# W_self's first row halves between x's tiles, their low halves on GpSimd, and the first products in another order

## The chip, the cores and the metric

The kernel runs on one core of one Trainium2 chip. The time is the device time of one execution in microseconds (us). The kernel before takes 241.03 us, the median of three runs (240.89 to 241.05). Differences of over 0.2% of that, 0.48 us, count as faster or slower here.

## The reference, cut to what matters

A graph layer over 625 nodes with 512 features and 20,625 edges of 4 kinds:

```python
h = relu(layernorm(x))
msg  = sum over r of (h[src] @ W_rel[r] + b_rel[r]) * where(edge_type == r, edge_weight, 0)
agg  = segment_sum(msg, dst) / max(segment_sum(edge_weight, dst), 1)
x1   = layernorm(h + h @ W_self + b_self + agg) * ln1_g + ln1_b
ffn  = gelu(x1 @ W_ffn1 + b_ffn1) @ W_ffn2 + b_ffn2
out  = x + layernorm(x1 + ffn) * ln2_g + ln2_b
```

Everything is float32. The change lies in the product `h @ W_self` and in what leads to it: the load of x, its row means and its transposition.

## The kernel before, in words

The 625 rows are five tiles of 125 (`c` or `s` from 0 to 4). An operand of a product is split in two float32r parts, a high one (a copy that rounds) and a low one (the rest), and a product is three: high by high, low by high, high by low. The low by low one is left out.

The weights come in units of 512 KB, two blocks of 128 rows of W (`k` = 0 and 1). Unit `u` lands in one of three staging buffers (`stage_view(u)`), ScalarE (ACT) writes its high part into `wring` (`high_part`), and VectorE (DVE) the low part (`low_part`). Units 0 and 1 are W_self; units 2 to 9 are W_rel; then come W_ffn1 and W_ffn2. Unit 0 is treated by itself: its two row halves are two DMAs of 256 KB, and each has its own conversion. The semaphore `first_in` tells that half 0 has landed and `stage_in[0]` that half 1 has; `first_hi`, `w_hi`, `first_lo` and `w_lo` tell of the conversions.

A tile of x goes this way: DVE takes its mean (`row_mean(c)`, three instructions), ACT subtracts it and applies the relu (`h_of(c)`), TensorE (PE) transposes it in four instructions (`turn_h(c)`), ACT writes the high part of the transposed tile (`hT_high(c)`) and DVE the low part (`hT_low(c)`), which give the semaphores `hT_a` and `hT_b`. Each engine does its work in the order in which the program writes it, and waits in that order. On ACT, `h_of(3)` stands behind `hT_high(2)`, and `h_of(4)` behind `hT_high(3)`.

PE starts with ten dummy products on a tile of ones, turns tiles 0 and 1, does three more dummies, and then the 30 products of unit 0, six for each tile, with the other three turns between them. Unit 1 follows at once. In the text a product is named by its two operands (the transposed h first), so high by low is hT's high part by W's low part, and by the row half and the tile: `(k, s)`.

GpSimd (POOL) fills constants until 6.2 us and has nothing to do until the five means are there. The loads are all issued by SyncE (SP), but for the last 13 rows of each tile of x, which ACT issues.

Of the kernel before, what the change touches and what calls it, by code (L numbers as in the profile page):

```python
# [10 lines left out]
ALU = mybir.AluOpType  # L11
# [8 lines left out]
def gnn_layer(nc, x, src, dst, etype, ew, W_self, b_self, W_rel, b_rel, ln1_g, ln1_b, ln2_g, ln2_b,  # L20
# [53 lines left out]
    RING = 2  # L74
    FG = [(0, 3 * TP), (3 * TP, 2 * TP)]
    UB = 6
    WARM = [10, 3]

    SUM_ROWS = [0, 32, 64]
    BK = SUM_ROWS[-1] + TR  # L80
# [96 lines left out]
    with ctx:  # L177
# [112 lines left out]
        def stage_view(u):  # L290
            v = stage[u % STAGES][:, :]
            return v if U_REL <= u < U_W1 else v.rearrange("p (k n) -> p k n", k=2)

        def f32(ap):
            return ap.bitcast(F32)
# [56 lines left out]
        @block.sync  # L352
        def _(sp):

            def load_x(c):
                p0, p1 = SPANS[0]
                sp.dma_start(x1[p0:p1, c, :], x[c * TN + p0:c * TN + p1, :]).then_inc(x_in[c], 16)  # L357

            def load(u):
                if u >= STAGES:  # L360
                    sp.wait_ge(w_lo, u - STAGES + 1)
                sp.dma_start(stage_view(u), units[u][0]).then_inc(stage_in[u % STAGES], 16)

            def sums_by_relation(c):

                sp.wait_ge(A_a, group_of(c, NG - 1))
                sp.wait_ge(A_b, group_of(c, NG - 1))
                if c >= 2:
                    sp.wait_ge(agg_ps, c - 1)
                for row, half in zip(SUM_ROWS, (0, 1, 0)):  # L370
                    sp.dma_start(f32(sums[row:row + TR, c % 2, :]),
                                 f32(AT[c % 2][half][SUMS:SUMS + 1, :, :])).then_inc(sums_in[c % 2], 16)

            for c in range(3):
                load_x(c)
            sp.dma_start(stage_view(0)[:, 0, :], units[0][0][:, 0, :]).then_inc(first_in, 16)  # L376
            sp.dma_start(stage_view(0)[:, 1, :], units[0][0][:, 1, :]).then_inc(stage_in[0], 16)
            for c in range(3, NT):
                load_x(c)
            load(1)  # L380
            sp.wait_ge(tails, 1)
            for f, vec, signal in ((1, dst, dst_in), (3, ew.bitcast(I32), w_in), (0, src, src_in), (2, etype, src_in)):
                flat = vec.rearrange("(p e) -> p e", p=TN)
                sp.dma_start(raw[0:TN, f, 0:EC], flat).then_inc(signal, 16)
                sp.dma_start(raw[0:TN - 1, f, EC:EW], flat[1:TN, 0:EW - EC]).then_inc(signal, 16)
            load(2)
            for buf, vec in ((bself_bc, b_self), (g1_bc, ln1_g), (b1_bc, ln1_b)):
                row = vec.rearrange("(a d) -> a d", a=1)
                sp.dma_start(buf[:, :], row.broadcast_to([P, D])).then_inc(consts_in, 16)
            with nc.allow_non_contiguous_dma("bias by partition"):  # L390
                sp.dma_start(bf1, b1.rearrange("(f p) -> p f", p=P)).then_inc(consts_in, 16)
            sp.wait_ge(blk_iotas, 3)
            for row in SUM_ROWS:
                for r in range(R):
                    sp.dma_start(brel_raw[row + r * NT:row + (r + 1) * NT, :],
                                 b_rel[r:r + 1, :].broadcast_to([NT, D])).then_inc(brel_in, 16)
            for u in range(STAGES, U_REL):
                load(u)
            sums_by_relation(0)
            for u in range(U_REL, U_REL + STAGES):  # L400
                load(u)
            for c in range(1, NT):
                sums_by_relation(c)
            for u in range(U_REL + STAGES, NU):
                load(u)

            sp.wait_ge(agg_ps, NT)
            for c in range(NT):
                for p0, p1 in SPANS:
                    sp.dma_start(x_again[p0:p1, c, :], x[c * TN + p0:c * TN + p1, :]).then_inc(late_in, 16)  # L410
            for buf, vec in ((g2_bc, ln2_g), (b2_bc, ln2_b), (bf2_bc, b2)):
                row = vec.rearrange("(a d) -> a d", a=1)
                sp.dma_start(buf[:, :], row.broadcast_to([P, D])).then_inc(late_in, 16)
            for c in range(NT - 1):
                sp.wait_ge(y_out, c + 1)
                for p0, p1 in SPANS:
                    sp.dma_start(out[c * TN + p0:c * TN + p1, :], ybuf[p0:p1, c % 2, :]).then_inc(out_done[c % 2], 16)
            p0, p1 = SPANS[0]
            for i, (d0, d1) in enumerate(HALVES):
                sp.wait_ge(y_out, NT + i)  # L420
                sp.dma_start(out[(NT - 1) * TN + p0:(NT - 1) * TN + p1, d0:d1],
                             ybuf[p0:p1, (NT - 1) % 2, d0:d1]).then_inc(last_done, 16)
            for i in range(2):
                sp.wait_ge(out_done[i], ROWS_IN * len(range(i, NT - 1, 2)))
            sp.wait_ge(last_done, 16 * 2 * len(HALVES))

        @block.gpsimd
        def _(pool):
            chain = [0]

            def link(ins):
# [29 lines left out]
            g.iota(iota_q[:, :, :], [[K_STEP, TR], [1, SW]], base=0, channel_multiplier=0,  # L461
                   allow_small_or_imprecise_dtypes=True).then_inc(iotas, 1)

            pool.wait_ge(xmean, NT)
            link(g.tensor_scalar(var_e, mv[:, :, 1], EPS, None, ALU.add))
            g.tensor_tensor(rstd, var_e, mhalf, ALU.pow).then_inc(xrstd, 1)
# [11 lines left out]
        def _(act):  # L478
# [12 lines left out]
                    act.wait_ge(agg_ps, NT)  # L491
                a.copy(units[u][1], stage_view(u)).then_inc(w_hi, 1)

            def first_high(k):

                if k == 0:
                    act.wait_ge(first_in, 16)
                    a.copy(units[0][1][:, 0, :], stage_view(0)[:, 0, :]).then_inc(first_hi, 1)
                else:
                    act.wait_ge(stage_in[0], 16)  # L500
                    a.copy(units[0][1][:, 1, :], stage_view(0)[:, 1, :]).then_inc(w_hi, 1)  # L501

            def h_of(c):

# [35 lines left out]
            h_of(0)  # L540
            h_of(1)
            hT_high(0)
            first_high(0)
            hT_high(1)
            first_high(1)
            h_of(2)
            hT_high(2)
            h_of(3)
# [65 lines left out]
        def _(dve):  # L614
# [16 lines left out]
            def row_mean(c):  # L631
                link(row_stats(c))
                link(v.bn_aggr(mv[0:TN, c, :], stats[0:TN, c, :]))
                v.tensor_scalar(nm[0:TN, c:c + 1], mv[0:TN, c, 0:1], -1.0, None, ALU.mult).then_inc(xmean, 1)

            def hT_low(c):
# [8 lines left out]

            row_mean(0)
            row_mean(1)
            row_mean(2)
            hT_low(0)
            dve.wait_ge(first_hi, 1)  # L650
            v.tensor_tensor(units[0][2][:, 0, :], stage_view(0)[:, 0, :], f32(units[0][1][:, 0, :]),
                            ALU.subtract).then_inc(first_lo, 1)
            hT_low(1)
            row_mean(3)
            dve.wait_ge(w_hi, 1)
            v.tensor_tensor(units[0][2][:, 1, :], stage_view(0)[:, 1, :], f32(units[0][1][:, 1, :]),
                            ALU.subtract).then_inc(w_lo, 1)
            hT_low(2)
            row_mean(4)
            hT_low(3)  # L660
# [363 lines left out]
        def _(pe):  # L1024
            def mm(o, l, r, start, stop=False):
                return nc.tensor.matmul(o, l, r, start=start, stop=stop, skip_group_check=True)  # L1026
# [28 lines left out]
            def product_lo(u, s):  # L1055

                half, w = u % 2, wring[:, u % WRING, :, :, :]
                if s == 0:
                    pe.wait_ge(w_lo, u + 1)
                if s == 0 and u == 0:  # L1060
                    pe.wait_ge(first_lo, 1)
                for k in range(2):
                    i = mm(ps[0:TN, s, :], hT_all[:, half, 0, k, s, :], w[:, 1, k, :], False, half == 1 and k == 1)
                return i
# [2 lines left out]
                product_hi(u, s)  # L1067
                return product_lo(u, s)

            def first_product(k, s):  # L1070

                if s == 0 and k == 0:
                    pe.wait_ge(first_hi, 1)
                if s == 0 and k == 1:
                    pe.wait_ge(w_hi, 1)
                if k == 0:
                    pe.wait_ge(hT_a, s + 1)
                mm(ps[0:TN, s, :], hT_all[:, 0, 0, k, s, :], wring[:, 0, 0, k, :], k == 0)
                if k == 0:
                    pe.wait_ge(hT_b, s + 1)  # L1080
                mm(ps[0:TN, s, :], hT_all[:, 0, 1, k, s, :], wring[:, 0, 0, k, :], False)
# [91 lines left out]
            turn_h(0)  # L1173
            turn_h(1)
            dummies(WARM[1])
            first_product(0, 0)
            first_product(1, 0)
            turn_h(2)
            first_product(0, 1)
            first_product(1, 1)  # L1180
            product_lo(0, 0)
            turn_h(3)
            product_lo(0, 1)
            unit_product(0, 2)
            turn_h(4)
            unit_product(0, 3)
            unit_product(0, 4).then_inc(unit_done, 1)
# [97 lines left out]
                stages(False)  # L1285

            pe.wait_ge(xT_b, 3)
            pe.wait_ge(w_lo, U_W1)
            pe.wait_ge(xpad, 1)
            i = 0  # L1290
            for g in range(len(FG)):
# [19 lines left out]
                    last.then_inc(U_ps, 1)  # L1311
                    i += 1

            pe.wait_ge(w_lo, NU)
            for c in range(NT - 1):
                pe.wait_ge(U_b, KF if c < 3 else 2 * KF)
                if c == 2:
# [41 lines left out]
```

## Time and profile before

| | us |
|---|---|
| median of three runs | 241.03 |
| the profiled execution | 240.98 |
| its span | 239.2 |
| PE busy | 231.3 |
| DVE busy | 181.1 |
| ACT busy | 65.5 |
| GpSimd busy | 16.6 |

Some 1.8 us of the profiled execution lie outside the span. In the rows, "PE" is the stream of products and transpositions and "PEld" the loads of their stationary operand, which run beside it. A float32 dummy product on ones is two entries in the trace, and a product of unit 0 is one. The end of a PE entry lies after the start of the next; starts tell the pace. A merged row gives the start of the first of its instructions, the time to the end of the last, and their count.

### The profile page before, as it was taken

The page shows a single profiled execution, that of the slowest core. Times are in us where ns is not written, and L with a number is a line of the kernel's source. Part 1 is how long each engine was busy: PE and PEld are TensorE (multiplying, and loading weights), DVE is VectorE, ACT ScalarE, POOL GpSimd, SP SyncE. Part 2 cuts the span into 40 slices and gives each one's busy share as a digit, 9 for nine tenths or more (in the row PEclk, how much of TensorE's full clock was granted, in tenths as well). Part 3 has the DMA queues.
Part 4 walks back from the last instruction along what each step waited for, and adds up shares of the span by engine and source line. Part 5 has one row for each costly group of instructions (what it writes and reads, how often), then busy time and mean ns, then how long its engine had stood idle before and what let it go on. Part 6 is the DMA issues. An engine that isn't in the chain of part 4 may idle for free.

```text
span 239.2 us, 4100 instructions
## 1 busy us (share of the span) xinstructions
PE 231.3 (97%) x1691; PEld 192.2 (80%) x1691; DVE 181.1 (76%) x339; ACT 65.5 (27%) x87; POOL 16.6 (7%) x36
## 2 busy tenths in 40 slices
PE   8899999999999999999999999999999999999990
PEld 8588787777777778888888888878889999887790
DVE  3869769799987877778889798929528789755564
ACT  3752424255062043102102202403315543100000
POOL 8020000000000000000010020002000000011111
PEclk9999999999999999999999999999999999999999
DMA  6867610314005200000000000004600670001211
GB/s 196 220 206 116 265 69 0 96 30 151 0 3 181 88 0 3 0 7 1 3 5 3 0 8 0 3 5 134 217 3 0 215 223 1 0 3 52 61 58 43
DMA packets 10392, 15.95 MB, mean 67 GB/s; under 512 B 2946, under 2 KB 3696, under 8 KB 10370
## 3 DMA queue, kind: packets, MB, share of 16 engines
q1 hardware_dynamic: 10188, 15.49, 21.9%
q8 instruction: 15, 0.25, 0.4%
q10 hardware_dynamic: 182, 0.16, 0.3%
q14 instruction: 7, 0.06, 0.1%
HBM read 14.22 MB, written 1.28 MB: 65 GB/s over the span
## 4 chain that ended last, share of the span: by engine, by line
PE 91%; DMA 3%; issue 2%; DVE 1%; SPq 1%; POOL 0%; ACT 0%; POOLq 0%; DVEq 0%
PE ps L1026 90%; DMA stage<-in_L_gnn_W_self 3%; PE ps L1129 1%; PE ps L1033 1%; SPq L357 1%; POOL small L475 0%; DVE small L1010 0%; DVE t2buf L1009 0%; ACT wring L501 0%; POOLq L177 0%; DVE ybuf L1002 0%; SPq L376 0%; DVEq L177 0%; DVE small L991 0%; DVE small L993 0%
## 5 line engine op out<-in xcount | busy, mean ns | idle before, releaser
L1026 PE MATMUL ps<-wring,hT 128*125 128x512 f32 x300 | 73.2, 399 | 0.8 <-ACT wring L501 0.4
L1026 PEld LDWEIGHTS ps<-wring,hT 128*125 128x125 f32 x300 | 54.5, 185 | 14.3 <-ACT wring L501 0.7
L1026 PE MATMUL ps<-T_hi,AT_hi 125*125 125x512 f32 x100 | 40.0, 400 | 0.0
L1026 PE MATMUL ps<-T_lo,AT_hi 125*125 125x512 f32 x100 | 39.5, 395 | 0.0
L725 DVE TENSOR_TENSOR eqp<-iota_p,pairs 128x1638 f16<-128x1638 f16 x25 | 25.1, 1006 | 7.4 <-PE ps L1026 6.1
L1026 PE MATMUL ps<-T_hi,AT_lo 125*125 125x512 f32 x100 | 26.0, 404 | 0.0
L529 ACT CAST AT_hi<-ps 128x1500 fp32r<-128x1500 f32 (+1 forms) x10 | 12.4, 1236 | 47.2 <-PE ps L1026 47.2
L1026 PEld LDWEIGHTS ps<-kw,eqp 128*128 128x128 f16 x650 | 18.9, 97 | 4.9 <-issue 4.9
L1026 PEld LDWEIGHTS ps<-T_lo,AT_hi 125*125 125x125 f32 x100 | 18.5, 185 | 4.4
L1026 PEld LDWEIGHTS ps<-T_hi,AT_hi 125*125 125x125 f32 x100 | 18.5, 185 | 4.3
L1026 PEld LDWEIGHTS ps<-T_hi,AT_lo 125*125 125x125 f32 x100 | 17.7, 185 | 3.9
L1026 PE MATMUL ps<-kw,eqp 128*128 128x40 f16 (+1 forms) x650 | 20.7, 190 | 0.0
L737 DVE TENSOR_TENSOR kw<-keq,pairs 128x520 f16<-128x520 f16 x50 | 19.2, 425 | 0.9
L518 ACT ACTIVATE T_hi<-ps,small 125x512 fp32r<-125x512 f32 x20 | 13.8, 689 | 21.3 <-PE ps L1026 21.2
L1026 PE MATMUL ps<-x1T_hi,W_hi 128*128 128x378 f32 (+1 forms) x64 | 18.9, 311 | 0.0
L1026 PE MATMUL ps<-x1T_lo,W_hi 128*128 128x378 f32 (+1 forms) x64 | 18.7, 309 | 0.0
L797 DVE SCALAR_TENSOR_TENSOR T_lo<-ps,small,T_hi 125x512 fp32r<-125x512 f32 x20 | 14.2, 746 | 4.2 <-ACT T_hi L518 4.2
L1026 PE MATMUL ps<-W_hi,u_hi 128*125 128x512 f32 (+1 forms) x48 | 17.2, 358 | 0.0
L1026 PE MATMUL ps<-W_hi,u_lo 128*125 128x512 f32 (+1 forms) x48 | 17.1, 356 | 0.0
L1026 PE MATMUL ps<-W_lo,u_hi 128*125 128x512 f32 (+1 forms) x48 | 17.1, 356 | 0.0
L790 DVE TENSOR_TENSOR AT_lo<-ps,AT_hi 128x1500 fp32r<-128x1500 f32 (+1 forms) x10 | 14.6, 1455 | 3.1 <-ACT AT_hi L529 3.1
L470 POOL TENSOR_TENSOR small<-small 125x1 f32<-125x1 f32 x5 | 5.0, 1003 | 159.3 <-DVE small L825 159.3
(129 smaller groups left out, 278.7 us busy)
## 6 DMA issues: line engine op xcount, KB each, us to landing
stage<-in_L_gnn_W_rel SPq DMA_DIRECT2D x8, 512.0 KB, 3.7
stage<-in_L_gnn_W_ffn SPq DMA_DIRECT2D x8, 512.0 KB, 3.9
x<-in_x SPq DMA_DIRECT2D x5, 224.0 KB
x_again<-in_x SPq DMA_DIRECT2D x5, 224.0 KB
out<-ybuf SPq DMA_DIRECT2D x4, 224.0 KB
stage<-in_L_gnn_W_self SPq DMA_DIRECT2D x2, 256.0 KB, 5.8
stage<-in_L_gnn_W_self SPq DMA_DIRECT2D x1, 512.0 KB, 7.7
g_bc<-in_L_gnn_ln_g SPq DMA_DIRECT2D x2, 256.0 KB, 5.9
```

What stands on the lines that cost most here:

```text
L357: sp.dma_start(x1[p0:p1, c, :], x[c * TN + p0:c * TN + p1, :]).then_inc(x_in[c], 16)
L470: g.tensor_tensor(rs1[0:TN, c:c + 1], ve1[0:TN, c:c + 1], mhalf[0:TN, 0:1], ALU.pow).then_inc(ln1_r, 1)
L518: a.mul(T_hi[0:TN, r, s, :], ps[0:TN, s, :], rstd[0:TN, s:s + 1]).then_inc(T_a, 1)
L529: a.copy(AT[n % 2][0][:, :, i0 * BW:(i0 + nb) * BW].rearrange("p q (i d) -> p i q d", i=nb), A_banks(g)[:, :, 0:TR * BW].rearrange("p i (q ...
L725: v.tensor_tensor(eqp[0:EK, z, :, 0:OW].rearrange("e s (n z) -> e s n z", z=2), iota_p[0:EK, 0:OW].rearrange("e (n z) -> e n z", z=2).unsq ...
L737: i = v.tensor_tensor(kw[0:EK, z, part, :, :, :], keq[0:EK, :, :, :], pairs[0:EK, 2 + part, at, :].unsqueeze(2).broadcast_to([EK, SL, TR, ...
L790: v.tensor_tensor(lo[:, :, cols].rearrange("p q (i d) -> p i q d", i=nb), A_banks(g)[:, :, 0:TR * BW].rearrange("p i (q d) -> p i q d", q=TR),
L797: v.scalar_tensor_tensor(out=T_lo[0:TN, r, s, :], in0=ps[0:TN, s, :], scalar=rstd[0:TN, s:s + 1], in1=f32(T_hi[0:TN, r, s, :]), op0=ALU.mu ...
L1026: return nc.tensor.matmul(o, l, r, start=start, stop=stop, skip_group_check=True)
L1033: i = nc.tensor.transpose(h_bank(c)[:, k * P:k * P + TN], x1[0:TN, c, k * P:(k + 1) * P], ident[0:TN, 0:TN])
L1129: i = nc.tensor.transpose(TURN[:, k * P:k * P + TN], x1[0:TN, c, k * P:(k + 1) * P], ident[0:TN, 0:TN])
```

## The change

1. SP issues half 0 of unit 0 between tiles 1 and 2 of x (it was behind tile 2), and half 1 behind tile 2, where it was.
2. Half 0's high part is made by DVE (a copy, ahead of `hT_low(0)` and of `row_mean(2)`) and no longer by ACT. `hT_low(0)` moves ahead of `row_mean(2)`. Half 1's high part stays with ACT.
3. Both low parts of unit 0 are made by GpSimd (they were DVE's), each as soon as the high part is there. `w_lo` no longer counts unit 0, so every wait for it is one lower, and the load of unit 3 waits for GpSimd's two.
4. PE does one dummy product between the turns and the products, not three. Then all twelve products of tiles 0 and 1 come first, with the high-by-low ones last, then the turn of tile 2, its high part's products, the turn of tile 3, tile 2's last two products, and the turn of tile 4.

```diff
             def load(u):
-                if u >= STAGES:
-                    sp.wait_ge(w_lo, u - STAGES + 1)
+                if u == STAGES:
+                    sp.wait_ge(first_lo, 2)
+                if u > STAGES:
+                    sp.wait_ge(w_lo, u - STAGES)
...
-            for c in range(3):
+            for c in range(2):
                 load_x(c)
             sp.dma_start(stage_view(0)[:, 0, :], units[0][0][:, 0, :]).then_inc(first_in, 16)
+            load_x(2)
             sp.dma_start(stage_view(0)[:, 1, :], units[0][0][:, 1, :]).then_inc(stage_in[0], 16)
...
+            for k, (signal, done) in enumerate(((first_hi, 1), (w_hi, 1))):
+                pool.wait_ge(signal, done)
+                g.tensor_tensor(units[0][2][:, k, :], stage_view(0)[:, k, :], f32(units[0][1][:, k, :]),
+                                ALU.subtract).then_inc(first_lo, 1)
...
             hT_high(0)
-            first_high(0)
             hT_high(1)
-            first_high(1)
+            second_high()
             h_of(2)
...
             row_mean(0)
             row_mean(1)
+            dve.wait_ge(first_in, 16)
+            v.tensor_copy(units[0][1][:, 0, :], stage_view(0)[:, 0, :]).then_inc(first_hi, 1)
+            hT_low(0)
             row_mean(2)
-            hT_low(0)
-            dve.wait_ge(first_hi, 1)
-            v.tensor_tensor(units[0][2][:, 0, :], stage_view(0)[:, 0, :], f32(units[0][1][:, 0, :]),
-                            ALU.subtract).then_inc(first_lo, 1)
             hT_low(1)
             row_mean(3)
-            dve.wait_ge(w_hi, 1)
-            v.tensor_tensor(units[0][2][:, 1, :], stage_view(0)[:, 1, :], f32(units[0][1][:, 1, :]),
-                            ALU.subtract).then_inc(w_lo, 1)
...
             turn_h(1)
             dummies(WARM[1])
-            first_product(0, 0)
-            first_product(1, 0)
+            high_high(0, 0)
+            high_high(0, 1)
+            low_high(0, 0)
+            high_low(0, 0)
+            high_low(0, 1)
+            high_high(1, 0)
+            high_high(1, 1)
+            low_high(1, 0)
+            low_high(0, 1)
+            low_high(1, 1)
+            high_low(1, 0)
+            high_low(1, 1)
             turn_h(2)
-            first_product(0, 1)
-            first_product(1, 1)
-            product_lo(0, 0)
+            product_hi(0, 2)
             turn_h(3)
-            product_lo(0, 1)
-            unit_product(0, 2)
+            product_lo(0, 2)
             turn_h(4)
             unit_product(0, 3)
```

On PE, before, from the dummies behind the turn of tile 1 to the turn of tile 4 (`wring,hT` is a product of unit 0, `ident,x_60` a transposition; the waits are semaphores):

```order
L1026 MATMUL ps<-ones 128x128 x3
L1026 MATMUL ps<-wring,hT 125x512 [waits hT_a,first_hi]
L1026 MATMUL ps<-wring,hT 125x512 [waits hT_b]
L1026 MATMUL ps<-wring,hT 125x512 [waits w_hi]
L1026 MATMUL ps<-wring,hT 125x512
L1033 MATMUL ps<-ident,x_60 128x125 [waits hT_b,h_act]
L1033 MATMUL ps<-ident,x_60 128x125 x3
L1026 MATMUL ps<-wring,hT 125x512 [waits hT_a]
L1026 MATMUL ps<-wring,hT 125x512 [waits hT_b]
L1026 MATMUL ps<-wring,hT 125x512 x2
L1026 MATMUL ps<-wring,hT 125x512 [waits first_lo,w_lo]
L1026 MATMUL ps<-wring,hT 125x512
```

Behind these stand the turn of tile 3, eight products and the turn of tile 4. In the changed kernel, from the wait for half 1 on (five products stand ahead of these rows):

```order
L1025 MATMUL ps<-wring,hT 125x512 [waits w_hi]
L1025 MATMUL ps<-wring,hT 125x512 x2
L1025 MATMUL ps<-wring,hT 125x512 [waits hT_b]
L1025 MATMUL ps<-wring,hT 125x512
L1025 MATMUL ps<-wring,hT 125x512 [waits first_lo]
L1025 MATMUL ps<-wring,hT 125x512
L1032 MATMUL ps<-ident,x_60 128x125 [waits hT_b,h_act]
L1032 MATMUL ps<-ident,x_60 128x125 x3
L1025 MATMUL ps<-wring,hT 125x512 [waits hT_a]
L1025 MATMUL ps<-wring,hT 125x512
L1025 MATMUL ps<-wring,hT 125x512 [waits hT_b]
L1025 MATMUL ps<-wring,hT 125x512
```

Between the wait for half 1 and the turn of tile 2 there were two products and are now seven. Between the turns of tiles 2 and 3 there were six and are now four, which belong to tile 2 itself; between those of tiles 3 and 4 there were eight and are now two.

On DVE, in the changed kernel, from the second mean to the third `hT_low` (`x_60` is the tile of x, `wring<-stage_52` the copy of half 0):

```order
L637 TENSOR_SCALAR small<-small 125x1 [waits dchain]
L652 CAST wring<-stage_52 128x512 [waits first_in]
L641 TENSOR_TENSOR hT<-ps,hT 128x2x2x125 [waits hT_a]
L632 BN_STATS small<-x_60 125x6 [waits x_in2]
L636 BN_AGGR small<-small 125x2 [waits dchain]
L637 TENSOR_SCALAR small<-small 125x1 [waits dchain]
L641 TENSOR_TENSOR hT<-ps,hT 128x2x2x125 [waits hT_a]
L632 BN_STATS small<-x_60 125x6 [waits x_in3]
```

The copy stands where the third mean stood, and the two subtractions are gone from the row.

## Rows read from the trace of the kernel before

**Rows 1.** The page: busy us by engine (share); costliest group: busy, mean ns.

```profile
PE 231.3 (97%) x1691; PEld 192.2 (80%) x1691; DVE 181.1 (76%) x339; ACT 65.5 (27%) x87; POOL 16.6 (7%) x36
...
L1026 PE MATMUL ps<-wring,hT 128*125 128x512 f32 x300 | 73.2, 399 | 0.8 <-ACT wring L501 0.4
```

**Rows 2.** Who waited for whom, PE: us in total, times, longest.

```profile
...
PE ps L1026 <- ACT wring L501: 0.4, 1, 0.4
PE ps L1026 <- ACT wring L498: 0.3, 1, 0.3
PE ps L1033 <- ACT x L506: 0.2, 1, 0.2
```

**Rows 3.** PE in two stretches: us, PE busy (count), PEclk, DMA share, GB/s.

```profile
15.00:42.00 27.00, 27.00 (x142) 1.00 0.47 135
43.00:227.00 184.00, 184.00 (x1421) 1.00 0.15 47
```

**Rows 4.** The chain that ended last: start us, us, what.

```profile
2.56 6.09 DMA stage<-in_L_gnn_W_self
8.68 0.63 ACT wring L501
9.35 0.73 PE ps L1026 x2
```

**Rows 5.** PE in time: start us, us, engine line op out<-in xcount [idle before].

```profile
0.98 4.63 PE L1026 MATMUL ps<-ones 128*128 128x128 f32 x20 [0.98 <-POOL ones L438]
7.09 0.84 PE L1026 MATMUL ps<-ones 128*128 128x128 f32 x6
8.19 0.79 PE L1026 MATMUL ps<-wring,hT 128*125 128x512 f32 x2 [0.27 <-ACT wring L498]
9.98 0.65 PE L1033 MATMUL ps<-ident,x 125*128 125x125 f32 x4
10.38 1.68 PE L1026 MATMUL ps<-wring,hT 128*125 128x512 f32 x6
11.91 0.65 PE L1033 MATMUL ps<-ident,x 125*128 125x125 f32 x4
14.26 0.59 PE L1033 MATMUL ps<-ident,x 125*128 125x125 f32 x4
14.61 5.82 PE L1026 MATMUL ps<-wring,hT 128*125 128x512 f32 x24
```

**Rows 6.** ACT in time.

```profile
7.52 0.62 ACT L498 CAST wring<-stage 128x512 fp32r<-128x512 f32 x1 [0.51 <-DMA stage<-in_L_gnn_W_self]
10.66 0.58 ACT L511 CAST hT<-ps 128x500 fp32r<-128x500 f32 x1 [0.74 <-PE ps L1033]
11.14 0.72 ACT L506 ACTIVATE x<-x,small 125x512 f32<-125x512 f32 x1
```

**Rows 7.** DVE in time.

```profile
4.69 0.69 DVE L629 BATCH_NORM_STATS2 small<-x 125x6 f32<-125x512 f32 x1
6.76 0.69 DVE L629 BATCH_NORM_STATS2 small<-x 125x6 f32<-125x512 f32 x1 [0.97 <-DMA x<-in_x]
8.36 0.68 DVE L651 TENSOR_TENSOR wring<-stage,wring 128x512 fp32r<-128x512 f32 x1
11.28 0.68 DVE L638 TENSOR_TENSOR hT<-ps,hT 128x500 fp32r<-128x500 f32 x1
16.64 1.21 DVE L625 TENSOR_TENSOR wring<-stage,wring 128x1024 fp32r<-128x1024 f32 x1
```

**Rows 8.** DVE by line and form: busy us, mean ns, idle before.

```profile
L982 DVE CAST u_hi<-u 128x378 fp32r<-128x378 f32 x8 | 2.8, 352 | 0.3 <-ACT u L601 0.3
L982 DVE CAST u_hi<-u 128x252 fp32r<-128x252 f32 x8 | 2.3, 286 | 0.7 <-ACT u L601 0.7
```

**Rows 9.** GpSimd in time.

```profile
2.26 0.52 POOL L447 MEMSET brel_raw<- 128x512 f32 x1
13.37 1.21 POOL L466 TENSOR_TENSOR small<-small 128x5 f32<-128x5 f32 x1
```

More of the change, by code:

```diff
@@ L76, in gnn_layer @@
     UB = 6
-    WARM = [10, 3]
+    WARM = [10, 1]
     SUM_ROWS = [0, 32, 64]
@@ L492, in high_part, with second_high @@
                 a.copy(units[u][1], stage_view(u)).then_inc(w_hi, 1)
[L494 to L501, printed above, removed]
+            def second_high():
+                act.wait_ge(stage_in[0], 16)
+                a.copy(units[0][1][:, 1, :], stage_view(0)[:, 1, :]).then_inc(w_hi, 1)
             def h_of(c):
@@ L1058, in product_lo @@
                 if s == 0:
-                    pe.wait_ge(w_lo, u + 1)
-                if s == 0 and u == 0:
-                    pe.wait_ge(first_lo, 1)
+                    pe.wait_ge(w_lo, u)
                 for k in range(2):
@@ L1068, in unit_product, with high_high @@
                 return product_lo(u, s)
-            def first_product(k, s):
+            def high_high(k, s):
                 if s == 0 and k == 0:
@@ L1078, in first_product, with high_low, low_high @@
                 mm(ps[0:TN, s, :], hT_all[:, 0, 0, k, s, :], wring[:, 0, 0, k, :], k == 0)
+            def high_low(k, s):
+                if s == 0:
+                    pe.wait_ge(first_lo, k + 1)
+                mm(ps[0:TN, s, :], hT_all[:, 0, 0, k, s, :], wring[:, 0, 1, k, :], False)
+            def low_high(k, s):
                 if k == 0:
@@ L1287, in _ @@
             pe.wait_ge(xT_b, 3)
-            pe.wait_ge(w_lo, U_W1)
+            pe.wait_ge(w_lo, U_W1 - 1)
             pe.wait_ge(xpad, 1)
@@ L1312, in _ @@
                     i += 1
-            pe.wait_ge(w_lo, NU)
+            pe.wait_ge(w_lo, NU - 1)
             for c in range(NT - 1):
```

## The prediction

> **What bounds the kernel now.** I read the busy times first. PE is busy for 231.3 of 239.2 us [rows 1], and no other engine comes near. Then who PE waits for: three waits behind its start, the longest for ACT's conversion of W_self's second row half, at 9.35 us [rows 2, 4]. From 15 to 42 us and from 43 to 227 us PE is busy for the whole stretch, 211 of 211 us [rows 3]. So whatever moves PE's products after the turn of tile 4 (the product at 14.61 us [rows 5]) moves the end by as much, in both directions: nothing downstream can absorb a delay, and a gain is kept only if no other engine becomes late. The question is only when that product starts, 14.61 us before. In the changed kernel as many products of unit 0, eighteen, stand ahead of it.
>
> The pace of PE comes from the same rows. Twenty-four products take 5.82 us, and an entry is 0.40 long and overlaps the next [rows 1]: (5.82 - 0.40) / 23 = 0.236 us each. The two products of 9.35 us are followed by the turn at 9.98: 0.63, not 0.47, so the first product behind an idle stretch costs 0.16 more. A turn costs 0.40 (9.98 to 10.38; 11.91 to about 12.3), or 0.35 if PE didn't idle before it (14.26 to 14.61) [rows 4, 5].
>
> **Up to the wait for half 1.** SP now issues half 0 where tile 2 of x stood, with 256 KB for 224. Tile 1 has landed by 4.69 us and tile 2 by 6.76, half 0 by 7.52 [rows 6, 7]. I take the 2.07 us between tiles 1 and 2 for the slot, and 0.1 for the extra bytes: half 0 lands at about 6.85, tile 2 at about 7.5. The bytes ahead of half 1 are the same, so it lands at 8.65 as before (2.56 + 6.09) [rows 4]; I bound a shift of it by 0.5 us on either side. DVE's copy is not in the trace at this size. By two other forms it costs (352 - 286) / 126 = 0.52 ns a column, so 352 + 134 x 0.52 = 422 ns for 512 columns [rows 8]. Half 0's high part is there at 7.27, where it was at 8.14 (7.52 + 0.62) [rows 6]. PE starts its first product at about 7.3 and not at 8.19. The two dummy products that go are no loss, since they filled idle time and the remaining one ends at about 7.3.
>
> From there, high by high (0,0) runs at 7.3, (0,1) at about 7.9 (it waits for the second `hT_high`, which ACT can do at 7.3 since half 0 is no longer in its way), low by high (0,0) at 8.2, and high by low (0,0) waits for GpSimd.
>
> GpSimd's subtraction of 128x512 has no row. Below, it can't do better than DVE's 0.68 us for the same form [rows 7]. Above: its two-operand row is 1.21 us for five columns of another function; if all of that were a fixed part, with two reads and a write behind it at the 0.52 us of a 512-column fill each, it would be 1.21 + 3 x 0.52 = 2.8 us [rows 9]. I take 1.2: that row is the nearest in kind, and a function of five columns that takes 1.21 is likely dearer by itself than a subtraction, which leaves room for the columns. By the Trainium skill, GPSIMD Engine Reference (Performance versus the Vector engine), a float32 add of 2048 columns takes 4497 ns at about 2.6 cycles a column, which scaled to 512 columns is an estimate of 1.2 us; no row here shows it.
>
> So the first low part is there at 7.27 + 0.1 + 1.2 = 8.57, and high by low (0,0) and (0,1) run at 8.6 and 9.0, before 9.35. Half 1's high part comes from ACT as before, and PE passes the wait for it at 9.35 in both kernels. At that moment two products had been done; now five have. Three products are worth 3 x 0.236 = 0.71 us, if they can be kept.
>
> **From half 1 to the turn of tile 2.** Before, two products and the turn at 9.98. Now seven: 9.35 + 0.16 + 7 x 0.236 = 11.16. The last two of them need GpSimd's second subtraction: 9.30 + 0.1 + 1.2 + 0.05 = 10.65, and PE reaches them at 9.35 + 0.16 + 5 x 0.236 = 10.69, so it is just hidden. The turn of tile 2 starts 1.18 us later than it did.
>
> **The turns of tiles 3 and 4.** Here I expect the loss. A turned tile has to go through ACT and back before the next one can be turned: turn at 9.98, ACT's high part at 10.66 for 0.58, ACT's relu of tile 3 at 11.14 for 0.72, next turn at 11.91 [rows 5, 6]. That loop is 1.93 us, and PE waited 0.2 us for it [rows 2] with six products between the turns. Now four and two stand there, worth 0.94 and 0.47 us, and the four are products of the very tile that has just been turned. Step by step:
> the high part of tile 2 is ready at 11.16 + 0.68 + 0.58 = 12.42. The two high products start at 12.47 and take 0.63, to 13.10. The low part: DVE 12.46 to 13.14 (0.68 [rows 7]), PE at 13.19; two products take up to 0.63, and the turn of tile 3 starts at 13.82. Two products follow and end their issue at 14.7. The turn of tile 4 has to wait for the loop: 13.82 + 1.93 = 15.75. The product behind it starts at 15.75 + 0.40 = 16.15, against 14.61: 1.54 us later.
>
> In idle time: from the turn of tile 2 to the product at 12.47 about 0.9 us, and from 14.7 to 15.75 about 1.05 us. The 1.54 is these 1.95 us, the small waits and restarts (0.3), less the three products done earlier (0.71).
>
> **What follows it.** Unit 1's low part is DVE's at 16.64 + 1.21 = 17.85 [rows 7]; PE asks for it sixteen products behind 14.61, at 18.4, so 0.55 us are in hand. Its DVE work stands behind `hT_low(4)`, which shifts with the turn of tile 4 by about 1.5, as PE does, so the margin stays. DVE loses two subtractions of 0.68 and gets a copy of 0.42: 0.94 us less on an engine that isn't the bound, and worth nothing. The load of unit 3 now waits for GpSimd at 10.65, long before SP gets to it. GpSimd's power for the row scale waits for all five means and is far from needed. All these cost nothing.
>
> **The sum.** 240.98 us for the profiled execution, plus 1.54, is 242.5. That execution stands 0.05 us below the median of the runs, which is nothing at this size.
>
> **Rivals.**
> A. Faster: the turns are hidden. If PE never waited after 9.35, it would do thirteen products and three turns: 9.35 + 0.16 + 13 x 0.236 + 1.2 = 13.78, which is 0.83 us before 14.61, so 240.15. For it: PE idles 0.3 and 0.4 us for the two conversions [rows 2], and it is true that three products move into that time. Against: it decides at a loop through ACT no longer than the products between two turns, 0.94 and 0.47 us, and the row shows 1.93. Chance 0.08.
> B. Slower still: GpSimd is slow. At 1.85 us the second low part comes at 11.3 and the turn of tile 2 at 12.0, 0.8 later than above: 243.3. At 2.8 us the first comes at 10.2, after PE's place for it, the second at 13.0, and the turn at 13.6, 2.4 later: 245. It decides from 1.2 us on. For it: GpSimd's rows are long for what they do [rows 9]. By the Trainium skill, SBUF — State Buffer, GpSimd and VectorE share a port pair that one of them holds for a whole instruction; by its conditions DVE's work in that time (one SBUF input each) wouldn't hold it, and if it did, B's times would be reached by waiting. Chance 0.14.
> C. The clock. PE's first twenty passes over ones take 4.63 us, 0.23 each, and six later ones 0.84, 0.14 each [rows 5]. The later pace is that of the 2.4 GHz level, the first looks like the 1.2 GHz level. From 15 us on the granted clock is 1.00 [rows 3]. The idle stretches of 0.9 and 1.05 us could bring the slow level back. A stretch as long as the first, 4.6 us, would do half its products: 2.3 us more, 244.8. Against: PE idled 0.3 and 0.4 us within 1.5 us [rows 2] and the pace behind them stayed full (six products in 1.68 us [rows 5]). The Trainium skill, TensorE: Matmul & The Clock Gate (Part 1), says that the gate halves the clock by how busy PE has been. Chance 0.05.
> D. The landings fall otherwise: with half 1 landing 0.5 us earlier, PE is held by GpSimd's first result and gains about 0.3; with GpSimd near 0.7 and shorter restarts, the loss shrinks to some 0.5, within what a measurement tells from none. Chance 0.05.
>
> **Chances.** The forecast holds 0.68, with its own range of 241.9 to 243.1: half 1's landing by half a microsecond, and the restarts. A is faster; D is the same; forecast, B and C are slower: 0.87. For A and D I give 0.08 and 0.05. The range for 8 in 10 reaches to B's first price and takes the low end down to where D begins: 241.4 to 243.5.
>
> **What would show it.** PE's first product near 7.3 us. ACT's conversion of half 1 still at 8.7, PE's sixth product at 9.35. GpSimd's two subtractions near 1.2 us. The turn of tile 2 at 11.2, tile 3 at 13.8, tile 4 at 15.75, and PE's waits for `hT` (ACT) and for x (ACT) in the list, near 0.9 and 1.0 us, where only 0.2 stood. From 16.2 us on no wait at all. A turn of tile 4 before 14.3 would prove me wrong, as would waits that PE makes good later.

## The result and the profile after

The changed kernel takes 242.65 us (median of six runs, 242.47 to 243.13), the kernel before 240.91 in runs on the same chips: a ratio of 1.0068 (95% interval 1.0056 to 1.008), slower by 1.7 us. The profiled execution took 242.47 us, 1.49 over that of before, and its span is 240.7.

PE in order of time, from the turn of tile 1 on (columns as in [rows 5], which are its counterparts):

```profile
7.02 0.39 PE L1025 MATMUL ps<-ones 128*128 128x128 f32 x2
7.16 0.47 PE L1025 MATMUL ps<-wring,hT 128*125 128x512 f32 x1
7.84 1.20 PE L1025 MATMUL ps<-wring,hT 128*125 128x512 f32 x4 [0.21 <-ACT hT L515]
9.31 2.10 PE L1025 MATMUL ps<-wring,hT 128*125 128x512 f32 x7 [0.26 <-ACT wring L505]
11.24 0.59 PE L1032 MATMUL ps<-ident,x 125*128 125x125 f32 x4
12.50 1.45 PE L1025 MATMUL ps<-wring,hT 128*125 128x512 f32 x4 [0.67 <-ACT hT L515]
13.79 0.59 PE L1032 MATMUL ps<-ident,x 125*128 125x125 f32 x4
14.14 0.71 PE L1025 MATMUL ps<-wring,hT 128*125 128x512 f32 x2
15.67 0.65 PE L1032 MATMUL ps<-ident,x 125*128 125x125 f32 x4 [0.82 <-ACT x L510]
16.07 2.11 PE L1025 MATMUL ps<-wring,hT 128*125 128x512 f32 x8
```

Read the starts of the three turns (the `ident,x` rows): 11.24, 13.79 and 15.67, where before had 9.98, 11.91 and 14.26. Ahead of the first stand five products of half 0 and, from 9.31 on, seven more. PE then stands idle twice: behind the turn of tile 2, for that tile's high part, and ahead of the turn of tile 4, for ACT's relu of it. The product behind the last turn starts at 16.07 instead of 14.61, 1.46 us later. The execution is 1.49 longer, so nearly all of it is there at 16 us. What PE waited for, in the form of [rows 2]:

```profile
PE ps L1032 <- ACT x L510: 1.2, 2, 0.8
PE ps L1025 <- POOL ones L441: 1.0, 1, 1.0
PE ps L1025 <- ACT hT L515: 0.9, 2, 0.7
PE ps L1025 <- ACT wring L505: 0.3, 1, 0.3
```

The wait for x was 0.2 us and is 1.2. Both figures hold a wait ahead of the turn of tile 1 (0.23 us at 6.60 before, 0.34 at 6.53 now); new is the 0.82 ahead of the turn of tile 4. The 0.9 for `hT`'s high part is new, 0.21 ahead of the second product and 0.67 behind the turn of tile 2. The 1.0 for `ones` is the start, as before. ACT, whose rows answer to [rows 6]:

```profile
8.63 0.62 ACT L505 CAST wring<-stage 128x512 fp32r<-128x512 f32 x1 [0.84 <-DMA stage<-in_L_gnn_W_self]
9.16 0.72 ACT L510 ACTIVATE x<-x,small 125x512 f32<-125x512 f32 x1
11.87 0.58 ACT L515 CAST hT<-ps 128x500 fp32r<-128x500 f32 x1 [1.99 <-PE ps L1032]
12.34 0.72 ACT L510 ACTIVATE x<-x,small 125x512 f32<-125x512 f32 x1
14.42 0.58 ACT L515 CAST hT<-ps 128x500 fp32r<-128x500 f32 x1 [1.35 <-PE ps L1032]
14.89 0.72 ACT L510 ACTIVATE x<-x,small 125x512 f32<-125x512 f32 x1
```

ACT stands idle for 1.99 us while PE does its seven products ahead of the turn of tile 2, and for 1.35 until the turn of tile 3. Behind these PE waits for ACT: each engine has other work in the program, but none that its order puts there. GpSimd and DVE, for [rows 7 and 9]:

```profile
6.93 1.28 POOL L469 TENSOR_TENSOR wring<-stage,wring 128x512 fp32r<-128x512 f32 x1 [0.71 <-DVE wring L652]
9.33 1.29 POOL L469 TENSOR_TENSOR wring<-stage,wring 128x512 fp32r<-128x512 f32 x1 [1.12 <-ACT wring L505]
```

```profile
6.42 0.43 DVE L652 CAST wring<-stage 128x512 fp32r<-128x512 f32 x1 [0.70 <-DMA stage<-in_L_gnn_W_self]
18.11 1.22 DVE L628 TENSOR_TENSOR wring<-stage,wring 128x1024 fp32r<-128x1024 f32 x1
```

GpSimd's second low part is there at 10.62, a little too late. The loads of PE's stationary operand, which run ahead of the products, show the wait:

```profile
10.68 0.29 PEld L1025 LDWEIGHTS ps<-wring,hT 128*125 128x125 f32 x2 [0.37 <-POOL wring L469]
```

The last two of the seven products start at 10.68 and 11.01, where their pace would have put them at 10.58 and 10.82: that is 0.2 us of the turn's delay, and the list of PE's waits doesn't have it. Unit 1's low part starts at 18.11 instead of 16.64, 1.47 later, as PE does. From there on the stretches of [rows 3] show no further loss:

```profile
15.00:42.00 27.00, 26.33 (x131) 1.00 0.54 132
43.00:227.00 184.00, 183.86 (x1442) 1.00 0.16 48
```

What is missing in the first is the idle time up to 15.67. The 0.14 in the second was there before too, but ahead of 43 us: PE's short stop of 0.13 us that ended at 42.70 now ends at 44.17.

### The profile page after: what moved, and what is told of

The parts are those of the page before. It is cut to its first block, busy times and chain, and to the rows that moved or that the text cites. A ratio compares the mean times of both kernels' runs of the same rounds, so it can differ in the third digit from the quotient of the medians.

```text
span 240.7 us, 4091 instructions
## 1 busy us (share of the span) xinstructions
PE 231.3 (96%) x1687; PEld 191.4 (80%) x1687; DVE 180.5 (75%) x338; ACT 65.2 (27%) x86; POOL 19.2 (8%) x38
## 3 DMA queue, kind: packets, MB, share of 16 engines
HBM read 14.22 MB, written 1.28 MB: 64 GB/s over the span
## 4 chain that ended last, share of the span: by engine, by line
PE 86%; DVE 5%; issue 3%; DMA 3%; ACT 1%; SPq 1%; POOL 0%; POOLq 0%; DVEq 0%
PE ps L1025 84%; DMA stage<-in_L_gnn_W_self 3%; PE ps L1133 1%; PE ps L1032 1%; SPq L357 1%; ACT hT L515 0%; DVE wring L628 0%; DVE eqp L724 0%; POOL small L483 0%; DVE pairs L712 0%; DVE pairs L709 0%; DVE pairs L715 0%; DVE kw L736 0%; DVE T_lo L796 0%; DVE small L1009 0%
```

## The experiments

Times are medians. "Ratio" is to the kernel before on the same chip (240.98 to 241.00 us there), with its 95% interval. Differences from the changed kernel compare medians of different chips, and where they are under some 0.5 us the two intervals overlap.

**1. The conversions and loads as changed, PE's order of before** (several calls to a line here).

```diff
-            high_high(0, 0)
...
-            product_lo(0, 2)
+            high_high(0, 0); low_high(0, 0); high_high(1, 0); low_high(1, 0)
+            turn_h(2)
+            high_high(0, 1); low_high(0, 1); high_high(1, 1); low_high(1, 1)
+            high_low(0, 0); high_low(1, 0)
+            turn_h(3)
+            high_low(0, 1); high_low(1, 1); unit_product(0, 2)
             turn_h(4)
```

> The changed kernel with its loads and conversions (half 0 between tiles 1 and 2, DVE's copy, GpSimd's low parts, one dummy), but PE's products and turns in the order of before. Theory (the loss is the late and close turns of tiles 2, 3 and 4): turn of tile 2 at 9.9 us, of tile 3 at 11.9, the product behind the turn of tile 4 at 14.5; 240.8 to 241.0 us, no different from before. Rival (GpSimd's conversions or the swapped loads cost the time): it stays within 0.3 us of the changed kernel, 242.3 to 242.8.

Measured: 241.2 us, ratio 1.0013 (1.0001 to 1.0026). It is 1.45 us below the changed kernel and 0.2 above before. So the order on PE carries most of the loss, and the rival falls as to its size. In its profiled execution half 1 came late (ACT took it at 9.07 us, before at 8.68) and the turns with it, but they are as far apart as before (1.93 and 2.36):

```profile
9.74 0.73 PE L1025 MATMUL ps<-wring,hT 128*125 128x512 f32 x2 [1.28 <-ACT wring L505]
10.38 0.65 PE L1032 MATMUL ps<-ident,x 125*128 125x125 f32 x4
10.78 1.64 PE L1025 MATMUL ps<-wring,hT 128*125 128x512 f32 x6
12.31 0.65 PE L1032 MATMUL ps<-ident,x 125*128 125x125 f32 x4
12.71 2.12 PE L1025 MATMUL ps<-wring,hT 128*125 128x512 f32 x8
14.67 0.59 PE L1032 MATMUL ps<-ident,x 125*128 125x125 f32 x4
```

**2. PE's order as changed, all else as before.** The same edit the other way round: the twelve products first, `turn_h(2)`, `product_hi(0, 2)`, `turn_h(3)`, `product_lo(0, 2)`, `turn_h(4)`, in the kernel before, with `high_low(1, 0)` waiting for DVE's subtraction.

> The kernel before with nothing changed but PE's order between the turns of tiles 1 and 4, which is the changed kernel's. Theory: high by low of half 1 has to wait for DVE's second subtraction, which ends at 11.3 us, so the turn of tile 2 starts at 12.0, 0.7 later than in the changed kernel, and the loop does the rest: 243.1 us. Rival (GpSimd or the loads cost the time): 241.0.

Measured: 243.08 us, ratio 1.0084 (1.0069 to 1.01). The order alone makes the whole loss and, by the medians, 0.4 us more; in the traces the product behind the last turn, at 16.43, is 0.36 later than in the changed kernel. The turns stand at 11.62, 14.15 and 16.03 us, the first 0.4 earlier than expected, so that the time came out at the forecast partly by luck. The wait for DVE is in the trace, its product 0.3 us earlier than expected:

```profile
11.05 0.73 PE L1026 MATMUL ps<-wring,hT 128*125 128x512 f32 x2 [0.25 <-DVE wring L656]
```

**3. The loop through ACT cut.**

```diff
             h_of(2)
-            hT_high(2)
             h_of(3)
-            hT_high(3)
+            hT_high(2)
             h_of(4)
+            hT_high(3)
             hT_high(4)
...
             row_mean(3)
-            hT_low(2)
             row_mean(4)
+            hT_low(2)
```

> The changed kernel with the loop through ACT cut: the mean of tile 4 ahead of the low part of tile 2 on DVE, the relu of tile 3 ahead of the high part of tile 2 on ACT, and that of tile 4 ahead of the high part of tile 3. PE's order is unchanged. Theory: the turn of tile 3 stays at 13.8 us, that of tile 4 no longer waits and starts at 14.7, the product behind it at 15.1 instead of 16.07: 241.6 us, one us below the changed kernel, and still 0.6 over before. Rival (the clock, GpSimd, or the products themselves): within 0.3 us of the changed kernel.

Measured: 241.96 us, ratio 1.004 (1.0025 to 1.0055): 0.7 below the changed kernel, not 1.0. PE's order is untouched, and the wait ahead of the last turn is gone:

```profile
12.38 1.44 PE L1025 MATMUL ps<-wring,hT 128*125 128x512 f32 x4 [0.67 <-ACT hT L515]
13.66 0.59 PE L1032 MATMUL ps<-ident,x 125*128 125x125 f32 x4
14.01 0.70 PE L1025 MATMUL ps<-wring,hT 128*125 128x512 f32 x2
14.55 0.59 PE L1032 MATMUL ps<-ident,x 125*128 125x125 f32 x4
```

The last two turns are now 0.89 us apart, where 1.88 stood. In its trace the product behind the turn stands at 14.92, 1.15 us before 16.07. Part of that is lost again to tile 3's products, which now stand right behind tile 3's parts: the starts behind the last turn are 0.34, 0.37 and 0.34 us apart instead of 0.31 once and 0.24, which is 0.26 in all. The 0.67 behind the turn of tile 2 stays, since those are tile 2's own products.

**4. The turns spread.**

```diff
+            def of_tile(s, part_h, part_w):
+                pe.wait_ge(hT_b if part_h else hT_a, s + 1)
+                for k in range(2):
+                    mm(ps[0:TN, s, :], hT_all[:, 0, part_h, k, s, :], wring[:, 0, part_w, k, :],
+                       k == 0 and part_h == 0 and part_w == 0)
...
             high_high(1, 1)
+            turn_h(2)
             low_high(1, 0)
             low_high(0, 1)
             low_high(1, 1)
             high_low(1, 0)
             high_low(1, 1)
-            turn_h(2)
-            product_hi(0, 2)
+            of_tile(2, 0, 0)
             turn_h(3)
-            product_lo(0, 2)
+            of_tile(2, 1, 0)
+            of_tile(2, 0, 1)
+            of_tile(3, 0, 0)
             turn_h(4)
-            unit_product(0, 3)
+            of_tile(3, 1, 0)
+            of_tile(3, 0, 1)
```

> The changed kernel with another order on PE: five products that need only half 0 as now, then two of half 1, the turn of tile 2, five more, tile 2's two high products, the turn of tile 3, six products, the turn of tile 4. Theory: turns at 9.95, 12.0 and 14.0 us, each as early as the loop through ACT allows, with no wait over 0.2 us, and 20 products ahead of the product at 14.4, where before had 18 ahead of 14.61: 240.2 us, 0.7 below before. Rival (three products can't be kept, since something downstream is late then, such as unit 1's low part, which had 0.55 us in hand, or the choice of the edges' groups on DVE): 240.7 to 241.

Measured: 241.03 us, ratio 1.0001 (0.9988 to 1.0014). The loss of the change is gone, 1.6 us by PE's order alone, but not the gain that I expected on top. Its execution had half 1 late (first product 9.77) and turns at 10.40, 12.52 and 14.40. The product behind starts at 14.80 with twenty done. Two starts behind it are 0.38 and 0.33 apart: tile 4's low part, which PE now reaches too early. The counts explain it: 14.80 against 14.61 is 0.19 later, two products more done are 0.47, and 0.24 is lost to that wait, so 0.04 is left. PE's product for the weight sum starts at 20.24, before at 20.26.

**5. The turn of tile 2 in the gap** (the edit is against experiment 4).

```diff
             hT_high(1)
+            h_of(2)
             second_high()
-            h_of(2)
             hT_high(2)
...
             high_low(0, 1)
+            turn_h(2)
+            low_high(0, 1)
             high_high(1, 0)
             high_high(1, 1)
-            turn_h(2)
             low_high(1, 0)
-            low_high(0, 1)
             low_high(1, 1)
-            high_low(1, 0)
-            high_low(1, 1)
             of_tile(2, 0, 0)
             turn_h(3)
+            high_low(1, 0)
+            high_low(1, 1)
             of_tile(2, 1, 0)
```

> The spread order again, with the turn of tile 2 moved into the idle time ahead of half 1's products: on ACT the relu of tile 2 goes ahead of half 1's conversion; on PE the five products of half 0, the turn of tile 2, low by high (0,1), four products of half 1, tile 2's two high products, the turn of tile 3, eight products, the turn of tile 4. Theory: turns at 9.4, 11.6 and 14.0 us, half 1's first product at 10.0, twenty products done at 14.4, whether half 1 lands at 8.6 or at 9.1 us: 240.3 us. Rival (what is gained ahead of 14 us is lost behind it, on DVE's or ACT's work for unit 1 or the edges): 240.9 to 241.2.

Measured: 240.83 us, ratio 0.9996 (0.9983 to 1.0008). The stretch itself came as expected: turns at 9.64, 11.75 and 14.03, the product behind at 14.38. The time did not: it can't be told from before. The profiled execution was 240.76.

**6. The spread order with the loop cut as well** (experiments 4 and 3 together).

> The spread order with the loop through ACT cut as well (relu of tile 3 ahead of the high part of tile 2, that of tile 4 ahead of the high part of tile 3, the mean of tile 4 ahead of the low part of tile 2). Theory: the loop no longer binds once six or seven products stand between two turns, so it saves only the 0.2 us wait ahead of the turn of tile 4, and some of that is lost to the wait for tile 4's low part: 240.7 to 241.0 us, against 241.03 with the spread order alone. Rival (the loop still costs what it did): 0.8 us less, 240.2.

Measured: 241.1 us, ratio 1.0005 (0.999 to 1.002). No gain beside the 241.03 of experiment 4, and the rival's 0.8 us is not there. That fits experiment 4's own trace, in which PE has no listed wait for x behind the turn of tile 1: with six and seven products between the turns, the loop is covered. The experiment is not clean, though. With the relu of tile 3 ahead of it, the high part of tile 2 comes later, and PE waits for that instead:

```profile
12.23 0.50 PE L1025 MATMUL ps<-wring,hT 128*125 128x512 f32 x1 [0.31 <-ACT hT L515]
```

**7. Experiment 1 with the loads of before.**

```diff
-            for c in range(2):
+            for c in range(3):
                 load_x(c)
             sp.dma_start(stage_view(0)[:, 0, :], units[0][0][:, 0, :]).then_inc(first_in, 16)
-            load_x(2)
             sp.dma_start(stage_view(0)[:, 1, :], units[0][0][:, 1, :]).then_inc(stage_in[0], 16)
```

> PE's order of before with DVE's copy and GpSimd's low parts, and SP's order of before (half 0 behind tile 2 of x). Theory A (the swap of the loads makes half 1 land up to 0.4 us later in some executions): half 1 has landed by 8.7 us and PE's first product of it starts at 9.35, and the time is 240.9 us, 0.3 below the 241.2 of the same kernel with swapped loads. Theory B (the landing scatters by itself, whatever the order): 241.2 again.

Measured: 241.24 us, ratio 1.0008 (0.9996 to 1.002), as with swapped loads. Theory A has no support in the time, though half 1 did land early here (ACT took it at 8.19). The trace shows something else that holds this kernel up: DVE takes the mean of tile 2 behind the copy and the low part of tile 0, so ACT's relu of tile 2 comes at 9.28 and PE waits for it ahead of the turn.

```profile
7.71 1.88 PE L1024 MATMUL ps<-wring,hT 128*125 128x512 f32 x4 [0.21 <-DVE wring L651]
10.05 0.65 PE L1031 MATMUL ps<-ident,x 125*128 125x125 f32 x4 [0.46 <-ACT x L509]
```

By the product behind the turn of tile 4 (14.70) that is 0.09 us of the 0.25 by which this execution is longer than before's; the rest comes later.

**8. Tile 4's low part last**, on top of experiment 5: high by high and high by low of tile 4 first, low by high behind them.

```diff
-            unit_product(0, 4).then_inc(unit_done, 1)
+            pe.wait_ge(hT_a, NT)
+            for part in range(2):
+                for k in range(2):
+                    mm(ps[0:TN, 4, :], hT_all[:, 0, 0, k, 4, :], wring[:, 0, part, k, :], part == 0 and k == 0)
+            pe.wait_ge(hT_b, NT)
+            for k in range(2):
+                i = mm(ps[0:TN, 4, :], hT_all[:, 0, 1, k, 4, :], wring[:, 0, 0, k, :], False)
+            i.then_inc(unit_done, 1)
```

> The order with the turn of tile 2 in the gap, and tile 4's six products with its low part last (high by high, high by low, then low by high), so that PE does not reach tile 4's low part before DVE has made it. Theory: the two starts 0.37 and 0.34 us apart behind the turn of tile 4 become 0.24, which is 0.24 us off: 240.6 us, 0.4 below before. Rival (DVE's work for unit 1 and the edges sets the pace by then): 240.8 as without it.

Measured: 240.7 us, ratio 0.9989 (0.9979 to 0.9999), 0.3 us below before. It is the only kernel here whose whole interval lies below 1, by a hair and as one of ten tried, and the difference is under the 0.48 us that count as faster: a gain of a few tenths is likely, not established. It can't be told from experiment 5 by the times either. In the trace both starts are 0.24 apart again, and the eleven products behind the turn run through:

```profile
9.62 0.65 PE L1032 MATMUL ps<-ident,x 125*128 125x125 f32 x4 [0.42 <-ACT x L510]
10.02 1.92 PE L1025 MATMUL ps<-wring,hT 128*125 128x512 f32 x7
11.78 0.59 PE L1032 MATMUL ps<-ident,x 125*128 125x125 f32 x4
12.13 2.09 PE L1025 MATMUL ps<-wring,hT 128*125 128x512 f32 x8
14.06 0.59 PE L1032 MATMUL ps<-ident,x 125*128 125x125 f32 x4
14.41 2.80 PE L1025 MATMUL ps<-wring,hT 128*125 128x512 f32 x11
```

**9. The changed kernel with the low parts on DVE.**

```diff
-            for k, (signal, done) in enumerate(((first_hi, 1), (w_hi, 1))):
-                pool.wait_ge(signal, done)
-                g.tensor_tensor(units[0][2][:, k, :], ...
...
             hT_low(0)
+            dve.wait_ge(first_hi, 1)
+            v.tensor_tensor(units[0][2][:, 0, :], ...
             row_mean(2)
             hT_low(1)
+            dve.wait_ge(w_hi, 1)
+            v.tensor_tensor(units[0][2][:, 1, :], ...
```

> The changed kernel with both low parts of unit 0 made by DVE again (the first behind the low part of tile 0, the second behind that of tile 1), all else as changed. Theory: DVE ends the second at 10.5 us, ahead of PE's place for it at 10.7, so the turns stay where they are: 242.6 us. Rival (GpSimd's 1.28 us a piece is part of the loss): 0.3 us or more below the changed kernel.

Measured: 242.7 us, ratio 1.0072 (1.0057 to 1.0086), the changed kernel's time, so handing the low parts to GpSimd rather than DVE changes nothing that can be measured. That is not because both come in time. In this execution half 0's copy began only at 7.39, DVE's second subtraction ended at 11.19 and not at 10.5 as in the theory, and PE was held up as by GpSimd in the changed kernel:

```profile
11.24 0.29 PEld L1026 LDWEIGHTS ps<-wring,hT 128*125 128x125 f32 x2 [0.30 <-DVE wring L655]
```

So the rival falls as to its 0.3 us, and the 0.2 us of the changed kernel's trace remains; what an earlier low part would be worth in the median isn't shown.

**10. The changed kernel with the loads of before** (the edit of experiment 7).

> The changed kernel with SP's order of before (half 0 behind tile 2 of x), all else as changed. Theory: half 0 lands at 7.2 to 7.5 us, GpSimd's first low part is there at 9.1, and half 1's first product starts at 9.6 and not 9.3; the turn of tile 2 at 11.4: 242.8 us, 0.2 over the changed kernel. Rival (the swap delays half 1 and with it everything): 242.2.

Measured: 243.14 us, ratio 1.0089 (1.0074 to 1.0103), 0.5 over the changed kernel, more than the 0.2 expected. Half 0's copy began only at 7.89, and GpSimd held PE:

```profile
8.37 1.08 PE L1024 MATMUL ps<-wring,hT 128*125 128x512 f32 x3 [0.72 <-DVE wring L651]
9.74 2.36 PE L1024 MATMUL ps<-wring,hT 128*125 128x512 f32 x9 [0.29 <-POOL wring L468]
```

The swap of the loads is thus worth 0.4 to 0.5 us in this order by the medians (243.14 against 242.7 for experiment 9 and 242.65 for the changed kernel), and the rival (it does harm) falls.

## Why the prediction was right, point by point

The forecast was 242.5, the profiled execution 242.47 and the median 242.65.

- Up to half 1: the first product was forecast at 7.3 and started at 7.16. Half 0 was there at 6.42 and not 6.85, so that PE's own turn of tile 1 and dummy product set that start. DVE's copy took 0.43 (0.42 forecast), GpSimd's subtraction 1.28 (1.2). The sixth product started at 9.31 (9.35). Right.
- The turn of tile 2: 11.24 for 11.16. Seven products behind the wait instead of two. Right, but the prediction had GpSimd's second result "just hidden", and it cost 0.2 us. A start 0.04 earlier and a slightly quicker restart and pace make up for a little over half of it.
- The turns of tiles 3 and 4: 13.79 and 15.67 for 13.82 and 15.75; waits of 0.67 and 0.82 us where I had put 0.9 and 1.05 of idle time. These entries count from the modelled end of the product ahead, some 0.2 us later than its issue. The prediction named the list's lines with near 0.9 and 1.0 us; that they read 0.9 and 1.2 is partly chance, since each holds a wait from before 8 us. The product behind: 16.07 for 16.15. Right, and shown by experiments 1 to 4: the order alone gives the loss (2), without it most of it goes (1), cutting the loop takes the wait ahead of the last turn away (3), and spreading the turns takes all of it (4, 6).
- One reading behind it was wrong: "PE waited 0.2 us for it" takes the 0.2 us of [rows 2] for the loop through ACT. That wait stands at 6.60, ahead of the turn of tile 1:

```profile
6.60 0.65 PE L1033 MATMUL ps<-ident,x 125*128 125x125 f32 x4 [0.23 <-ACT x L506]
```

  No wait is listed at 11.91: before, six products and the loop of 1.93 us took just as long as each other. The sum doesn't use the 0.2, and the loop measured 1.88 (13.79 to 15.67).
- Nothing downstream absorbs it: 1.46 us at 16 us, 1.49 at the end. Right for this loss. In the other direction it isn't sure: experiment 5's execution was ahead by 0.45 us at 41 us and by 0.22 at the end.
- The 0.71 us of three early products "if they can be kept": the sum counts them as kept, as a credit against 1.95 and 0.3 of new idle time, and so did the kernel: five products were done at the wait for half 1, and the same eighteen stand ahead of the last turn. The credit was real, and outweighed.
- Rival A would have needed the turns hidden. Experiment 8 hides those of tiles 3 and 4, with another order on PE and ACT, and even then gets 0.3 us and not 0.8. B falls with the 1.28 us of GpSimd's subtraction, C with the pace behind the idle stretches (eight products in 2.11 us at 16.07, as before in 2.10 at 12.32). C reads the first twenty passes over ones as the 1.2 GHz level; the granted clock is given as 1.00 there too (0 to 5.3 us, both kernels), so that column doesn't bear it out. D falls with half 1's conversion at 8.63, before at 8.68.
- The median came out 0.25 us further from before than the profiled execution did (1.74 for 1.49). That the forecast sits 0.03 from the profiled time is luck at this size. The profiled one was the fastest of the six. That part isn't explained by a row; the last section has two things that scatter by such amounts.

What I had wrong of the experiments: 1, 3, 4, 5 and 10 were each forecast 0.2 to 0.8 us too fast. In 4, 0.24 us of the 0.8 was an oversight (tile 4's low part), which experiment 8 mended, and 0.4 is the product behind the turn of tile 4 at 14.80 for 14.4, with both halves landing late. In 9 the time was right and the path to it wrong. That the new conversions cost 0.2 us with the old order is itself barely clear of noise in 1 and not in 7. The late mean of tile 2 is in the trace of 7, worth 0.09 us there; in that of 1 the turns are late with half 1.

## What to carry to other kernels

When a change puts independent work ahead of a step that feeds a chain through other engines, price the chain, not the work: here three products gained 0.7 us and moving the turns back cost 2.2 (an estimate: the 1.46 measured and the 0.71). Give each round trip (here 1.93 us) enough work between its two ends, and not work that needs what the round trip is about to bring. Order on the bound engine by who waits for the result, the feeding step first.

## What the runs showed that I had not expected

- Landings scatter by as much as the effects here. With swapped loads DVE's copy of half 0 began between 6.36 and 7.39 us in eight profiled executions, and ACT took half 1 at 8.52 to 9.21 in the six of them in which it waited for that landing. With the loads of before it was 8.19 to 8.93 in four. The ranges overlap; whether the swap makes half 1 land later by some 0.3 us on average can't be told from ten executions. A forecast to 0.3 us needs more than one trace's landing.
- Behind PE's branch near 49 us stands an idle time that no engine's work explains (DVE has made the block by then). In PE's weight loads, before and experiment 1:

```profile
49.87 1.02 PEld L1026 LDWEIGHTS ps<-kw,eqp 128*128 128x128 f16 x31 [0.40 <-issue]
```

```profile
50.63 1.04 PEld L1025 LDWEIGHTS ps<-kw,eqp 128*128 128x128 f16 x36 [0.76 <-issue]
```

  In experiment 5 it is 0.58 and in experiment 8 0.54. That is where experiment 5's execution gave back 0.2 of the 0.45 us by which it was ahead (the first block's product at 41.24 for 41.69, the end at 240.76 for 240.98). Experiment 8's lost 0.1 there and was 0.6 ahead at the end all the same (240.37). Whether the place of the branch in time matters, or chance, stays open.
